# Value copy ahead of the exponentials, and four block transposes behind the first low parts, in a fused two-layer graph network on one core

## What is computed

```python
def layer0(x, adj):                       # HD = 32, 8 heads
    nx = ln(x, ln1_g, ln1_b)
    q, k, v = nx @ wq + bq, nx @ wk + bk, nx @ wv + bv
    bias = where(adj > 0, 0.1 * adj * adj, -inf)
    attn = softmax(q k^T / sqrt(HD) + bias)
    x1 = x + (attn @ v) @ wo + bo
    return x1 + gelu(ln(x1, ln2_g, ln2_b) @ w1 + b1) @ w2 + b2
def layer1(x, adj):
    sc = where(adj == 0, -inf, (x @ Wq) @ (x @ Wk)^T / 16)
    return layer_norm(x + softmax(sc) @ (x @ Wv) @ Wo + bo, gamma, beta)
```

## Time and profile before

| | us |
|---|---|
| median of 3 runs (lowest, highest) | 890.98 (890.16, 891.61) |
| the profiled execution, its own time | 891.15 |
| its span in the profile | 889.4 |
| busy in the span: PE, DVE, ACT, POOL | 853.3 (96%), 703.3 (79%), 609.6 (69%), 507.5 (57%) |

### The profile page before, as it was taken

The page is one execution under the profiler, slowest core; times in us unless marked ns, Lnnn a source line. Parts: engine busy times, 40 slices in busy tenths (PEclk is TensorE's granted clock), DMA queues, the critical chain, the costliest instruction groups (busy, mean ns, idle before and its releaser), DMA issues.

```text
span 889.4 us, 21938 instructions
## 1 busy us (share of the span) xinstructions
PE 853.3 (96%) x7059; PEld 754.3 (85%) x7059; DVE 703.3 (79%) x2548; ACT 609.6 (69%) x1830; POOL 507.5 (57%) x374
## 2 busy tenths in 40 slices
PE   8899797799999999999999999999999999999996
PEld 8787687589898989889898988989798988989795
DVE  6695777868888898888888797888889887875636
ACT  5684865667868676776768676786867677684542
POOL 3522743756666565775647566666656577655312
PEclk9899999799999999999999999999999999999998
DMA  8000245445536353444546343553635343343001
GB/s 272 16 24 13 66 105 187 129 152 136 177 94 200 101 180 99 127 154 114 181 118 189 106 146 105 138 176 95 200 96 182 86 124 120 99 143 115 24 1 36
DMA packets 131122, 107.32 MB, mean 121 GB/s; under 512 B 5750, under 2 KB 112908, under 8 KB 131084
## 3 DMA queue, kind: packets, MB, share of 16 engines
q1 hardware_dynamic: 131068, 106.85, 40.5%
q10 hardware_dynamic: 16, 0.00, 0.0%
HBM read 61.48 MB, written 45.35 MB: 120 GB/s over the span
## 4 chain that ended last, share of the span: by engine, by line
PE 74%; ACT 3%; DVE 3%; POOL 1%; issue 1%; DVEq 0%; POOLq 0%
PE bank L455 21%; PE bank L457 20%; PE bank L456 20%; PE bank L618 3%; PE bank L743 3%; PE bank L774 3%; PE bank L642 3%; ACT p L1116 2%; PE bank L724 1%; DVE p L1540 1%; PE bank L767 0%; POOL p_s L2013 0%; POOL x_bo L1983 0%; POOL x_b L1993 0%; DVE stats L1375 0%
## 5 line engine op out<-in xcount | busy, mean ns | idle before, releaser
L1052 ACT ACTIVATE p_s<-bank,neg_max 128x128 f32<-128x128 f32 x464 | 163.0, 391 | 78.2 <-DVE neg_max L1443 78.1
L2013 POOL TENSOR_TENSOR p_s<-p_s,rsum 128x512 f32<-128x512 f32 x116 | 118.1, 1041 | 73.9 <-DVE rsum L1450 52.2
L455 PE MATMUL bank<-w_hi,hT_hi 128*128 128x256 f32 x512 | 147.5, 288 | 1.3 <-DVE hT_lo L1316 1.3
L457 PE MATMUL bank<-w_hi,hT_lo 128*128 128x256 f32 x512 | 144.1, 281 | 0.0
L456 PE MATMUL bank<-w_lo,hT_hi 128*128 128x256 f32 x512 | 144.0, 281 | 0.0
L1443 DVE CUSTOM_DVE_ANT_0 bank<-bank,bias 128x128 f32<-128x128 f32 x464 | 117.4, 325 | 2.0 <-PE bank L618 1.5
L455 PE MATMUL bank<-n2T_hi,w_hi 128*128 128x512 f32 (+1 forms) x272 | 111.4, 409 | 5.1 <-DVE hT_lo L1316 5.1
L1083 ACT ACTIVATE bank<-bank,vec_cols 128x512 f32<-128x512 f32 (+1 forms) x136 | 86.5, 636 | 31.1 <-PE bank L457 22.5
L1052 ACT ACTIVATION_READ_ACCUMULATOR p_s<-bank,neg_max 128x1 f32 x464 | 107.1, 231 | 0.0
L456 PE MATMUL bank<-n2T_lo,w_hi 128*128 128x512 f32 (+1 forms) x272 | 105.2, 387 | 0.0
L457 PE MATMUL bank<-n2T_hi,w_lo 128*128 128x512 f32 (+1 forms) x272 | 105.1, 387 | 0.0
(11 more groups left out here) (242 smaller groups left out, 2432.6 us busy)
## 6 DMA issues: line engine op xcount, KB each, us to landing
parked<-pT SPq DMA_DIRECT2D x116, 256.0 KB, 3.8
pT<-parked SPq DMA_DIRECT2D x15, 1024.0 KB, 5.5
p_s<-parked SPq DMA_DIRECT2D x14, 1024.0 KB, 7.7
xs<-in_x SPq DMA_DIRECT2D x15, 512.0 KB, 3.9
out<-y SPq DMA_DIRECT2D x14, 512.0 KB, 3.0
x_bo<-in_x SPq DMA_DIRECT2D x13, 512.0 KB, 3.8
parked_x<-nx SPq DMA_DIRECT2D x48, 128.0 KB, 2.5
hT_hi<-parked_x SPq DMA_DIRECT2D x12, 512.0 KB, 5.0
```

Source lines behind the costliest of these rows:

```text
L455: mm(out, a_hi, b_hi, start=first, stop=False)
L457: return mm(out, a_lo, b_hi, start=False, stop=last)
L1052: last = run(to, of, ACT.Exp, scale=-1.0, bias=neg_max[:, r, place:place + 1], accum_out=psum[:, r, place:place + 1])
L2013: P.tensor_tensor(p_s[:, r, :, :], p_s[:, r, :, :], rsum[:, r, :, None].to_broadcast([128, 4, NODES]), ALU.mult).then_inc(pool_p, 1)
```

## The change

On ACT, at the end of the second turn, `v_copy(3, 1)` stands ahead of all four `exps(3, 1, r)` and no longer between the second and the third. On DVE, at the end of the second turn, the two `residual3(1, q)` stand ahead of the four `inverse(3, 1, r)`, and the four `blocks(3, 1, r)` leave this turn. They go into the third turn, which is taken out of DVE's loop and written with `turn(4, 3, 2, 1, 5)`: there the first four low parts of the hidden layer and the four transposes come right behind `nxT_low(4)`, and the first norm of group 5 (`sums1`, `moments`, `norm1`, `xblocks`), which stood among the low parts, comes behind all of them. DVE's loop starts at g = 4. PE, POOL and SP are as before; no work is added or dropped.

```diff
@@ ACT, second_turn
                 p1T_copy(1)
-                exps(3, 1, 0)
-                exps(3, 1, 1)
                 v_copy(3, 1)
-                exps(3, 1, 2)
-                exps(3, 1, 3)
+                for r in range(HPT):
+                    exps(3, 1, r)
@@ DVE, turn
                 nxT_low(gp)
+                third = isinstance(gp, int) and gp == 4
+                if third:
+                    h_low(gb, 0)
+                    h_low(gb, 1)
+                    blocks(3, 1, 0)
+                    blocks(3, 1, 1)
+                    h_low(gb, 2)
+                    blocks(3, 1, 2)
+                    blocks(3, 1, 3)
+                    h_low(gb, 3)
                 if gn is not None:
                     sums1(gn)
                     moments(1, gn)
-                h_low(gb, 0)
-                h_low(gb, 1)
+                if not third:
+                    h_low(gb, 0)
+                    h_low(gb, 1)
                 if gn is not None:
                     norm1(gn)
-                h_low(gb, 2)
+                if not third:
+                    h_low(gb, 2)
                 if gn is not None:
                     xblocks(gn)
-                h_low(gb, 3)
+                if not third:
+                    h_low(gb, 3)
                 h_low(gb, 4)
@@ DVE, second_turn
                 inverse_sums1(1)
-                for r in range(HPT):
-                    inverse(3, 1, r)
                 residual3(1, 0)
                 residual3(1, 1)
                 for r in range(HPT):
-                    blocks(3, 1, r)
+                    inverse(3, 1, r)
@@ DVE, the calls
             second_turn()
-            with dve.Fori(3, GROUPS - 3) as g:
+            turn(4, 3, 2, 1, 5)
+            with dve.Fori(4, GROUPS - 3) as g:
                 turn(g + 1, g, g - 1, g - 2, g + 2)
```

## The result

| | before | changed |
|---|---|---|
| median, us (8 runs of each, lowest to highest) | 891.21 (889.5 to 891.61) | 893.31 (892.02 to 894.66) |
| ratio, 95% interval | | 1.0027 (1.0016 to 1.0038) |
| profiled execution, its span | 891.15, 889.4 | 893.28, 891.5 |

In these runs the change makes the kernel about 2.1 us slower, though both gaps that it aimed at shrank or went. The first group of rows is PE's timeline of the changed kernel; it answers to the earlier trace rows.

The account below looks back on a forecast made before the run. PE was taken as the bound, with late parked-block loads gating group 3's attend. Late landing +0.5 and half clock +2.0 give +2.5 us: 893.65 against the profiled run, 893.5 against the median; range 890.0 to 895.7.

Parts of the forecast that it names:

- front of the turn: From first attend1 to group 3's attend: 2.10 us gap goes, 3.93 us gap becomes 3.0, PE ready 4.2 to 5.4 us earlier.
- divisions on POOL: POOL's divisions using the later inverses start at 162.87 anyway, behind a mask, and end at 166.9; cost nothing.
- parked path: Last transpose, then SP's stores and loads of pT and p_s, gate group 3's attend: 3.85 us later against 3.4 slack.
- landing: p_s, issued at 178.14, lands by 186.8 at a load of 8.7 us; second attend of group 3 starts +0.5 us.
- low end, 7.7: Load of p_s taking 7.7 us, as in the next turn, which puts the second attend of group 3 at -0.6 us.
- clock term: Half clock on PE behind the two waits at group 3's attend loses 2.0 us, between 0.35 and 2.8.
- Rival 3: Low parts behind group 5's norm, not the loads, hold PE at group 3's attend: +3.6 to +5 us, 895; chance 0.10.
- Rival 1: Loads land in time, p_s by 182, both old gaps mostly won: -4.2 to -5.4 us, 886.5; chance 0.13.
- straight code: DVE's third turn taken out of its loop: cost 0, up to +1 us if DVE stalls before the first low part.

Follow-up runs that it names:

- the run with nothing behind it: Changed kernel with two waits on SP ahead of its loop, so later stores and load go out only after both parked-block loads land: ratio 1.0001, 890.76 us.
- the other pair: Two profiles of the changed kernel with the four transposes put back ahead, among the first low parts: ratios 0.9978 (turn 60.52 us) and 0.9965 (turn 58.78 us).
- the version with the blocks ahead: Changed kernel with the four transposes of group 3 back ahead, among the first two low parts and before nxT_low: ratio 0.9965, 886.49 us; repeated 0.9978, 887.94 us.
- the three traces named: Changed kernel's first profile (1.0027), changed kernel with blocks 2 and 3 behind group 5's moments (1.0056), and the repeat with the four transposes back ahead (0.9978).

## Why the prediction was right
The forecast was 893.5, 0.28% over the kernel before; 893.31 and 1.0027 were measured. The mechanism was right: late loads, two waits at `attend` and half clock behind them. That the number came so close is in part luck. Point by point:

- The front of the turn went nearly as worked out. First `attend1` in one piece; gap ahead of the fifth `mlp_up` 3.0 us forecast, 3.19 measured; last block 15.24 us behind the first `attend1` forecast (171.5 - 156.26), 15.10 measured. The divisions on POOL, costed at nothing, ran beside `nxT_low`, which ended 10.71 us behind `attend1` and not 9.74 (166.0 - 156.26). PE was ready for `attend` at 25.39 behind `attend1` (182.84 - 2.05 - 155.40), just past the 23.8 to 25.0 of the forecast.
- The parked path was the gate. Slack 3.4 us against a move of 3.85: measured, the block moved by 3.71, and PE waits there 2.05 and 1.80 us, ended by DMAs. Transposes earlier and later moved the turn with them.
- The landing was right by two errors that cancel. Issue of `p_s` 6.60 us behind the first store forecast, 7.12 measured (170.53 to 177.65); load 8.7 taken, 8.0 measured. The sum, +0.5 us at the second `attend`, was +0.19 and -0.03 in the two traces. The argument for 8.7, a store close behind the load, was wrong: the run with nothing behind it puts its price at 0.1 to 0.3 us. The low end, 7.7, was the better row.
- The clock term was nearly right in size where it strikes: 2.0 us forecast, 1.6 measured (62.94 - 61.18, less 0.19; 60.52 - 58.78, less 0.16, in the other pair). I missed two things. It does not strike in every execution, though I took it as certain: the changed kernel's median moves from +2.1 to +1.3 us between two sets of runs. And where it strikes, a stretch of half clock in the last turn comes with it, 1.5 us that the sum had no term for. In the profiles 1.76 of the forecast's 2.5 us arose in this turn; the last turn's stretch, less the 0.86 us that this trace was ahead before the turn, brought the total to 2.1. So the sum was nearer to the first set than its reasoning deserved.
- Rival 3 did not decide: the low parts `h_low(2, 5)` to `h_low(2, 7)` came in one piece from 179.63 to 181.51, ahead of both loads. Rival 1, loads in time, is what the version with the blocks ahead makes true in part: -2 was its price for blocks through by 169, and the turn measured 2.4 us less.
- The straight code was taken at 0 and costs nothing.

## What to carry to other kernels
When a step is moved back to let another one go first, list what starts from it, DMAs above all, and set the length of that path against the slack at its end; here 3.7 us of move met 3.4 us of slack. Put first what starts a long transfer, then what feeds the next engine, then what nobody waits for soon; both could be had here. Here a short new wait on PE cost more in clock than in time, and not in every execution, and part of the cost lay in a turn that nobody had touched. So compare many runs, and look at the granted clock over the whole span before a difference of 2 us is put down to the code.

## What the runs showed of the hardware
- Half clock in some executions only: two waits of PE of 2.05 and 1.80 us were followed by half clock (from 186.1 to 189.5, with 182.84 to 186.1 still at full), and two of 2.12 and 1.60 us in the same kernel were not. One of 2.13 us, behind one of 0.62, was; one of 1.37 us was not. In the last turn the wait of 1.25 us ahead of the stretch shown was followed by half clock, 1.5 to 2.1 us after its end, in the three traces named, and in the nine others it was not. What decides isn't shown. With idle matmuls in the waits, 1.16 and 1.38 us of them, no execution's mean clock fell under 0.985, and the spread halved.
- `nxT_low`, a subtraction with both inputs in SBUF, took 1.25 us for two parts where POOL was through with its divisions, and 2.23 to 2.26 in the six traces of the changed order where it ran beside them (one part 1.52 instead of 0.65, two of POOL's divisions 1.49 and 1.48 instead of 1.04). With the blocks ahead it came behind them again and took 1.27. The Trainium skill says of this ("SBUF — State Buffer", Who interferes with whom) that a DVE operation with two SBUF inputs contends with a GpSimd operation that reads SBUF for one pair of ports, and that the one that starts later waits. The traces agree: both grew longer. The prediction had the first low part 0.4 us too early for it (10.24 us behind `attend1`, 10.63 measured).
- From the end of the last transpose to the issue of the first load, with four stores between, it took 6.2 us in the trace of before and 6.8 in the same order as straight code, 6.7 and 6.5 in the two traces of the changed kernel, and 7.3 (165.31 to 172.63), 7.4 and 6.5 with the blocks ahead. Why it differs stays open.
